# Experts' first product as seven block products with its weight sums on GpSimd, and the PSUM banks split anew, in a four-layer kernel

## The reference

```python
logits = (xt @ Wr + br) / TEMP
gates = entmax_bisect(logits)            # 25 bisection steps, 8 experts per token
gates = jnp.where(gates > THRESH, gates, 0.0)
h = jax.nn.relu(jnp.einsum('td,edf->etf', xt, W1) + b1[:, None, :])   # E=8, D=256, F=1024
y = jnp.einsum('etf,efd->etd', h, W2) + b2[:, None, :]
out = jnp.einsum('etd,te->td', y, gates)
...
s = _L1_attn_ref(xn, ...)                # Mamba-2: in-projection, conv of 4 taps, chunked scan, norm, out-projection
g = _silu(_L1_ffn_ref(xn, ...))
x = x + s * g
```

## Time and profile before

| | us |
|---|---|
| launches | 4301.44, 4306.74, 4305.99 |
| median | 4305.99 |
| the profiled execution, its span | 4303.7 |
| layer 1 in it, by PE | about 637 to 2756 |
| one sequence of layer 1, from the second on | 261.3 |
| PE busy in the span | 4153.6 (97%) |

### The profile page before, as it was taken

The page is one execution under the profiler, slowest core; times in us unless marked ns, Lnnn a source line. Parts: engine busy times, 40 slices in busy tenths (PEclk is TensorE's granted clock), DMA queues, the critical chain, the costliest instruction groups (busy, mean ns, idle before and its releaser), DMA issues. The chain is left out here.

```text
span 4303.7 us, 55507 instructions
## 1 busy us (share of the span) xinstructions
PE 4153.6 (97%) x19557; PEld 2428.1 (56%) x19557; DVE 2299.6 (53%) x5833; ACT 1638.2 (38%) x3132; POOL 307.1 (7%) x412
## 2 busy tenths in 40 slices
PE   7999988999999999999999999999998998999999
PEld 3444445666656667666666666656666554333333
DVE  6666645243242523415243252287787887666765
ACT  2444443223232232322223232354544321455555
POOL 0122210101011010100201001000000000000000
PEclk8999999999999999999999999999999999999999
DMA  3111101212211121121212112100000000111110
GB/s 88 17 17 17 35 26 60 90 59 81 79 70 72 57 100 70 65 85 59 81 68 85 66 69 90 56 1 1 1 1 14 8 1 22 19 22 22 26 24 22
DMA packets 52696, 198.22 MB, mean 46 GB/s; under 512 B 10256, under 2 KB 20144, under 8 KB 35384
## 3 DMA queue, kind: packets, MB, share of 16 engines
q1 hardware_dynamic: 51616, 194.57, 13.7%
q10 hardware_dynamic: 816, 0.20, 0.0%
HBM read 171.14 MB, written 4.46 MB: 41 GB/s over the span
## 5 line engine op out<-in xcount | busy, mean ns | idle before, releaser
L1146 PE MATMUL l_exp_out<-l_w,l_hidden 128*128 128x256 f32 x4096 | 907.0, 381 | 4.1 <-DVE l_moe L1484 3.7
L1136 PE MATMUL l_hid<-l_xn_t,l_w 128*128 128x512 f32 x2048 | 896.4, 594 | 0.8
L1146 PEld LDWEIGHTS l_exp_out<-l_w,l_hidden 128*128 128x128 f32 x4096 | 773.9, 190 | 124.3 <-DVE l_moe L1484 9.7
L1288 ACT ACTIVATE l_hidden<-l_hid,l_w 128x512 f32<-128x512 f32 x512 | 351.5, 687 | 927.2 <-PE l_hid L1136 927.2
L1136 PEld LDWEIGHTS l_hid<-l_xn_t,l_w 128*128 128x128 f32 x2048 | 386.1, 190 | 469.9 <-issue 447.9
L507 DVE TENSOR_REDUCE l3f_row_max<-l3f_bank 128x1 f32<-128x512 f32 x512 | 327.6, 685 | 176.9 <-PE l3f_bank L387 176.5
L463 ACT ACTIVATE l3f_prob_t<-l3f_bank 128x512 f32<-128x512 f32 x512 | 277.2, 596 | 206.2 <-PE l3f_bank L394 206.2
L1484 DVE SCALAR_TENSOR_TENSOR l_moe<-l_exp_out,l_gates,l_moe 128x256 f32<-128x256 f32 x256 | 123.7, 483 | 418.1 <-PE l_exp_out L1146 408.0
L504 DVE CUSTOM_DVE_ANT_0 l_masked<-l_bank,l_mask 128x256 f32<-128x256 f32 (+3 forms) x512 | 226.7, 487 | 160.6 <-PE l_bank L387 159.7
L394 PE MATMUL l3f_bank<-l3f_qk_t 32*128 32x512 f32 x1024 | 302.9, 637 | 0.9 <-ACT l3f_prob_t L463 0.5
L387 PE MATMUL l3f_bank<-l3f_qk_t 32*128 32x512 f32 x1024 | 297.2, 644 | 6.6 <-DMA l3f_qk_t<-l3f_packed 6.4
(11 more groups left out here) (485 smaller groups left out, 5640.9 us busy)
## 6 DMA issues: line engine op xcount, KB each, us to landing
l_w<-in_w SPq DMA_DIRECT2D x128, 1024.0 KB, 4.9
l_mix<-l_cum SPq DMA_DIRECT2D x32, 512.0 KB, 3.8
l_qk_t<-l_packed SPq DMA_DIRECT2D x128, 64.0 KB
l3f_qk_t<-l3f_packed SPq DMA_DIRECT2D x128, 64.0 KB
all_x<-in_x SPq DMA_DIRECT2D x8, 512.0 KB, 6.8
out_x<-all_x SPq DMA_DIRECT2D x7, 512.0 KB, 3.0
l_hidden<-in_fp4w SPq DMA_DIRECT2D x1, 2304.0 KB
l_qk_t<-l_max_rows SPq DMA_DIRECT2D x128, 2.0 KB
```

The source lines that it names most:

```text
L1136: ins = nc.tensor.matmul(bank[:, :], w1[:, e % 2, c, f * P:(f + 1) * P], xn_t[:, b % 2, c, :], start=c == 0, stop=c == CT - 1)
L1146: ins = nc.tensor.matmul(bank[:, 0:C], hidden[:, e % 2, f, j * P:(j + 1) * P], w2[:, e % 2, f, :], start=f == 0, stop=f == HF - 1)
L1288: hid.empty(nc.scalar.activation(hidden[:, e % 2, f, :], bank[:, :], ACT.Relu, bias=w[:, B1][:, e * HF + f:e * HF + f + 1]), (e, f))
```

## The change

**The product.** W1 of an expert (256 channels x 1024 features) and the input (256 channels x 512 tokens) are each cut in 2x2 blocks: 128 channels x 512 features, and 128 channels x 256 tokens. Eight block products give way to seven (Winograd's form of Strassen's scheme). Each of the seven is 4 matmuls of 128x128 weights on 256 columns, in two halves x = 0, 1 that fill one bank each. They are named by bank set and turn: a0, b0, a1, b1, a2, b2, a3, in that order on PE. a1, a2 and a3 add to what is in the banks of a0, b2 to b1; the partial results are read out between.

**Sums.** POOL makes four weight sums per expert (`weight_sums`, 128x512 each, float32) and four input sums per sequence (`input_sums`, 128x256 each).

**Draining.** ACT copies a0, a1 and b1 out to `hidden` (six of 128x512); DVE adds b0, a2 and b2 to these cells in place (`add_11`, `add_22`, `add_12`, six of 128x512); ACT then does bias and relu from SBUF (four of 256 columns, `relus_22`; four of 512, `relus_1`), and the last block straight from PSUM (four of 256, `relus_21`). Before, ACT had eight relus of 512.

**Banks.** `hid` has four banks, `ring` two instead of four, `exp_out` two as before. Expert e + 1 takes the sets a and b the other way round, so its a0 goes into the banks of b2 of expert e, its b0 into those of a3.

**Router.** The loop is unrolled; the halved widths are worked out ahead (`widths`), so a step has 7 instructions instead of 8. Of the 25 steps 14 lie where they lay before; the last 11 go 8, 2, 1 ahead of and between the adds of the next sequence's expert 0 (`begin`), with the gated update of x (`gate_all`, two of 128x1024) behind `add_12` of expert 0. In sequence 0 they go 9, 3, 3, 3, 3, 4.

**Order and buffers.** z comes ahead of xb; the silu of `moe` (L1356 before) comes behind z; the scan's transposes (`tokens`) are spread into `expert_out(1)`. The gates go through four transposes instead of one. W1 is loaded in halves of 512 KB, the first half into a single buffer as soon as a0 has read it and three of the sums are made. `x_tok` is gone, `s` lies in `mix[:, 1]`, so SP waits for `gate_all` ahead of that tile's load.

The diff, cut to its core:

```diff
+    hid = Jobs(a, [a.ps(f"hid{i}") for i in range(4)], "hid", products,
+               on=[2 * x + (e + (which == "b")) % 2 for e, x, which, _ in products])
-    banks = [a.ps(f"bank{i}") for i in range(4)]
+    banks = [a.ps(f"bank{i}") for i in range(2)]
...
-                def expert_in(e, features=range(HF)):
-                    pe.wait_ge(w1_loaded[e % 2], 16 * (b * (E // 2) + e // 2 + 1))
-                    for f in features:
-                        bank = hid.open(pe, b, (e, f))
-                        for c in range(CT):
-                            ins = nc.tensor.matmul(bank[:, :], w1[:, e % 2, c, f * P:(f + 1) * P], xn_t[:, b % 2, c, :],
-                                                   start=c == 0, stop=c == CT - 1)
-                        hid.fill(ins, (e, f))
+                def product(e, which, turn, weights, moving):
+                    for x in range(2):
+                        name = (e, x, which, turn)
+                        bank = hid.open(pe, b, name)
+                        for i in range(2):
+                            k = 2 * x + i
+                            ins = nc.tensor.matmul(bank[:, i * TH:(i + 1) * TH], weights[:, k * P:(k + 1) * P], moving,
+                                                   start=i == 0 and (which, turn) in (("a", 0), ("b", 0), ("b", 1)), stop=True,
+                                                   skip_group_check=True)
+                        hid.fill(ins, name)
+                    product(e, "a", 0, w1_first[:, 0:HALF_F], x_first[:, 0:TH])
+                    product(e, "b", 0, second[:, 0:HALF_F], x_second[:, 0:TH])
+                    product(e, "a", 1, sum_of(e, S2), x_sums[:, T2, :])
+                    product(e, "b", 1, sum_of(e, S1), x_sums[:, T1, :])
+                    product(e, "a", 2, sum_of(e, S3), x_sums[:, T3, :])
+                    product(e, "b", 2, sum_of(e, S4), x_second[:, TH:T])
+                    product(e, "a", 3, second[:, HALF_F:F], x_sums[:, T4, :])
...
+                def relus(e):
+                    relus_22(e)
+                    for x in range(2):
+                        relus_1(e, x)
+                        relus_21(e, x)
...
+                if n:
+                    hid.wait_filled(pool, before[0], (before[1], 1, "b", 1))
+                V.tensor_tensor(w1_sums[:, S1, :], high, second[:, HALF_F:F], ALU.add).then_inc(w1_summed, 1)
+                V.tensor_tensor(w1_sums[:, S2, :], w1_sums[:, S1, :], low, ALU.subtract).then_inc(w1_summed, 1)
+                V.tensor_tensor(w1_sums[:, S3, :], low, high, ALU.subtract).then_inc(w1_summed, 1)
+                V.tensor_tensor(w1_sums[:, S4, :], second[:, 0:HALF_F], w1_sums[:, S2, :], ALU.subtract).then_inc(w1_summed, 1)
...
+            def add(it, e, which, turn, half_f, half_t, copied):
+                for x in range(2):
+                    bank = hid.wait_filled(dve, it, (e, x, which, turn))
+                    hid.wait_emptied(dve, it, (e, x, *copied))
+                    cell = hidden_block(e, half_f, x, half_t)
+                    hid.empty(V.tensor_tensor(cell, pair(bank), cell, ALU.add), (e, x, which, turn))
...
-                    route(st, BISECT - 14)
-                    route_end(st)
-                    jobs.wait_emptied_through(dve, b, [f"o{j}" for j in range(TJ)])
-                    dve.wait_ge(gate_ready, b + 1)
-                    st.link(V.tensor_tensor(s[:, :, :], s[:, :, :], moe[:, :, :], ALU.mult))
-                    V.tensor_tensor(x_all[:, b], x_all[:, b], s[:, :, :], ALU.add)
+                    begin(st, b + 1, (8, 2, 1), gate_all)
```

More of the change, by code:

```diff
@@ new lines, in sequence @@
+                for name, weight in (("z", wz), ("xb", wx)):
+                    for f in range(FT):
+                        bank = jobs.open(pe, b, f"{name}{f}")
+                        for c in range(CT):
+                            ins = nc.tensor.matmul(bank[:, :], weight[:, c, f * P:(f + 1) * P], xn_t[:, b % 2, c, :],
+                                                   start=c == 0, stop=c == CT - 1)
+                        jobs.fill(ins, f"{name}{f}")
+                expert_in(0)
+                expert_in(1, {5: gates_in})
@@ L1283, in sequence @@
                 jobs = last_ring if is_last else ring
-                def relus(e, features=range(HF)):
-                    for f in features:
-                        bank = hid.wait_filled(act, b, (e, f))
-                        hid.empty(nc.scalar.activation(hidden[:, e % 2, f, :], bank[:, :], ACT.Relu,
-                                                       bias=w[:, B1][:, e * HF + f:e * HF + f + 1]), (e, f))
                 def copy_out(name, out, cols, rows=P):
@@ L1435, in route @@
[L1435 to L1447 removed]
+                st.link(V.tensor_scalar(mass_lo[:, :], mass[:, :], -1.0, None, ALU.add))
```

649 lines of the change are left out of this document (411 added, 238 removed).

## The result

The changed kernel takes 4258.95 us (median of 4 runs, 4254.05 to 4264.5) against 4306.36 us for the kernel before (4 runs, 4301.44 to 4308.87): a ratio of 0.9894, 95% interval 0.988 to 0.9908. That is 47 us less, where 77 were forecast (4229); the range of 4205 to 4272 holds it. The profiled execution spans 4257.2 us, before 4303.7.

A forecast was written before the change was run, and what follows sets the result against it. PE, busy 97% of the span, was taken as the bound, through columns streamed and waits. -105.0 - 7.0 + 2.3 (transposes) + 2.5 + 23.1 + 6.8 = -77.3 us, from 4306 to 4229; 8 in 10: 4205 to 4272.

The forecast's parts named there:

- clock or larger waits: Forecast band of 4243 to 4275 us, for half clock or longer PE waits than summed; chance 0.22.
- The product, -105: Expert products on PE: seven blocks take 12.18 us per expert, 1.64 less, 105.0 us less for 64 experts.
- the slower rival: PE's product: a bubble at each half block, 896 places, +90 (4319) or +170 us (4399); chance 0.11, 0.08 of it slower.
- the steady part costs nothing: Experts 3 to 7: ACT, DVE, POOL and W1's loads keep up with PE, at no cost.
- `expert_out(7)`, -7: Shorter bisection steps end DVE's lag in `expert_out(7)`: 1.0 us less in each of seven sequences.
- z first, +2.5: z with two banks: ACT's table load ahead of its first silu makes z2 wait 0.35 us, 2.5 in seven sequences.
- The seam, +23.1: Between experts 0 and 1, sequences 1 to 7: PE waits 3.3 us each, from 1.7 without collisions to 4.1.
- No collisions: Rival: DVE's bisection steps slip between POOL's sums, seam 1.7 us, sequence 0 and z nothing: 4208 us; chance 0.17.
- the rival at 4254: Seam: PE's clock falls after each 3 us of waiting, 2 to 4 us more each, +25 us; band's chance 0.22.
- Two ring banks: nothing: `ring` cut to two banks: each is emptied before it is wanted again, so no cost.
- That leaves over 1.6 us of slack at every bank: Product's banks, steady part: wanted again 2.6 us after full, and ACT or DVE empties them well before.
- Sequence 0, +6.8: Sequence 0: gates ready at 702.5, `expert_out(0)` starts about 710, 3.5 us later; correction plus 6.8 (bounds 0 and 12).

The follow-up runs named there:

- runs 1 and 2: Against the changed kernel: 1, POOL's weight sums cover 8 of 512 columns, 4237.14 us; 2, POOL's sums for expert 1 start only after a3, 4245.19 us.
- run 5: Changed kernel with the last sequence's 28 norm statistics taken in threes behind the sums of experts 2 to 4: 4248.4 us.
- early_pool: Changed kernel with POOL's wait for DVE's d_col moved behind its first four input sums and four weight sums: 4259.47 us.

## Why the prediction was right in direction and 30 us off

The measured 4259 us lie inside the stated range, but not in the forecast's own band (4215 to 4243, 0.50): they lie in the one for "clock or larger waits" (0.22), and some of what filled the gap is of neither kind.

- **The product, -105: right.** 12.18 us per expert as summed, from the 256-column tiles of the earlier trace rows, and no bubble at a wait; the slower rival was excluded by every `expert_in` of experts 3 to 7. The claim that the steady part costs nothing held, but for about 0.2 us at each place where a small product now stands between two tiles of `expert_out` (3.65 instead of 3.45 from start to start, 0.8 us a sequence in all, with the pieces' own).
- **`expert_out(7)`, -7: right.** 13.81 us, no wait for DVE.
- **z first, +2.5: not there.** z and xb take 13.73 us, as before; ACT's table load ends 33 us ahead of the first silu, in an idle stretch.
- **The seam, +23.1: right in its mechanism, small by 5.** 4.0 us a sequence instead of 3.3: waits of 2.48 + 0.18 + 0.76, and some 0.2 us more until PE is at pace behind each. That is the dear end (4.1), which the x_dt row spoke for: two of the sums fell into the last step. (The three waits without collisions, 0.2, 0.35 and 1.05, add up to 1.6 and not 1.7.) "No collisions" fell with runs 1 and 2.
- **Clock at the seam, the rival at 4254: its time came out near, for another reason.** One of the prediction's own signs of being wrong, 0.50 of the clock behind the seam, came in four of seven sequences, behind a wait of 2.47 us and not only of 11.26, but it cost only some 0.2 us there on average, as the periods show. A time that hits a rival's does not make it the cause.
- **"Two ring banks: nothing": the step that failed in every sequence.** It asked only when a bank is wanted and when it is empty. What four banks also gave was four row groups at once: +1.27 us in the bias products, 10 us in eight sequences. The operands' layout stood in the diff, and the 0.71 us for four products of 256 columns, well under the 1.74 of their eight records, in the trace.
- **DVE's order behind the bias products: a term that was missing.** `expert_out(0)` takes 14.2 to 14.3 us in sequences 1 to 6 and 13.92 in 0 and 7: about 0.3 us in six sequences, 2 us. What differs there is the turn of DVE's loop ahead of its first sum (last section); that the turn is the cause is argued from this, and no run moved it.
- **"That leaves over 1.6 us of slack at every bank": the step that failed in the last sequence.** It was worked out for a steady sequence. In the last one, 11.4 us of statistics stand ahead of an add, and an add now empties a bank of the product: 9.8 us (run 5).
- **Sequence 0, +6.8: 3.4 too small.** The bisection did not start at 650.0 but at 654.9: the router's start ahead of it takes 5.5 us instead of 1.8, since six of its instructions met POOL's first sums (2.0 us in `early_pool`, without them), and the whole layer began 0.7 us later. From there to the gates it was the 52.5 us of the sum, so they came at 707.4 instead of 702.5 (the terms as written add up to 702.1). `expert_out(0)` started at 715.3 instead of 710, but gave 1.9 us back, 13.92 instead of 15.84 at half clock, which the forecast did not count. Run 1 puts the collisions with the weight sums there at 8.7 us, where all together were taken at 5.

Sum of the misses: 10 (bias products) + 10 (last sequence) + 5 (seam) + 9 (small pieces and `expert_out(0)`) + 3 (sequence 0; its bias products are in the 10) + 1 (outside layer 1), less 7 (z, and 0.5 us a sequence that `expert_in(2)` gained beyond its columns): 31.

## What to carry to other kernels

When a second engine begins to empty the banks of the engine that bounds the kernel, go through that engine's whole order in every sequence, the first and the last above all: each long row of work on it that nobody waited for is now in the path. When banks are cut, look for products that ran beside each other in row groups, since their time goes up though no bank is ever waited for. And place an idle engine's long SBUF instructions where the other engine's tiny ones are not on the path: moving four sums by 5 us, without taking any away, gave 17 us in layer 1 and 14 in the median time. Last, when the start of a stretch that you measure can move, count from a point ahead of it: `early_pool` seems to gain 1.3 us only because its first product came later.

## What the runs showed of the hardware

- A DVE instruction with two SBUF operands beside a POOL sum lasts until that sum ends (0.19 us became 1.22). A reduction of an SBUF tile and an add with a PSUM operand don't wait (0.19 and 0.69 us as ever). One SBUF input alone is no safeguard: the TENSOR_SCALAR instructions L1618, L1620 and L1628 took 0.75, 0.42 and 0.90 us beside POOL's first sums, and 0.17 in `early_pool`. Where DVE's own instruction is long, POOL pays too: 2.14 and 2.25 us instead of 1.27.
- Four products of 8 rows and 256 columns: 0.65 us in four row groups and four banks, 1.06 in two and two, 1.92 in one row group and two banks.
- At the seam a wait of 2.47 us dropped the granted clock in four sequences and left it in three, with the same work around it; 5.4 us dropped it in all seven, 0.76 us and less in none.
- At the turn of DVE's loop 3.08 us lie between the last copy of an iteration and the first instruction of the next. Sequence 7 stands outside the loop, and there the same two instructions are 0.22 us apart, and `expert_out(0)` takes 13.92 us where sequence 3 has 14.30: the sum that frees its first bank stands behind the turn. What the engine does in the 3 us, the profile doesn't show. The first row is of sequence 3, the second of sequence 7:

```profile
1479.41 2.37 DVE L1725 TENSOR_SCALAR l_conv<-l_xbc,l_w 128x512 f32<-128x512 f32 x5 [3.08 <-issue]
...
2490.78 1.46 DVE L1725 TENSOR_SCALAR l_conv<-l_xbc,l_w 128x512 f32<-128x512 f32 x3 [0.22 <-DVE l_moe L1679]
```
